# Preparing one attention head at a time in the front of a two-layer cross-attention and feed-forward kernel: key and query side by side, one transpose for both

## What is computed

```python
# x: (2, 1024, 256), ctx_768: (2, 77, 192); 4 heads of 64
ln = layernorm(layernorm(x), ln_l_g, ln_l_b)            # "latents", 1024 tokens
xn = layernorm(ctx, ln_x_g, ln_x_b)                     # context, 77 tokens
q  = ln @ Wq.T
kv = concat([xn @ Wkv.T, ln @ Wlkv.T], axis=1)          # keys and values of 77 + 1024 tokens
k, v = kv[..., :256], kv[..., 256:]
qn, kn = rmsnorm(q, qn_g) * 64**-0.5, rmsnorm(k, kn_g)  # per head, over its 64 numbers
attn = softmax(where(mask, einsum('bhid,bhjd->bhij', qn, kn), -max))
x = x + einsum('bhij,bhjd->bhid', attn, v) @ Wo.T + bo
# then: x + ffn0(norm(x)); x + attention1(norm(x), ctx); x + experts(norm(x)), 8 experts
```

## Time and profile before

| | us |
|---|---|
| median of 3 runs | 837.75 |
| lowest, highest | 835.34, 842.58 |
| span of the profiled execution, first to last instruction | 832.3 |
| TensorE busy, VectorE busy | 766.2, 534.6 |
| ScalarE busy, GpSimd busy | 396.6, 303.0 |

### The profile page before, as it was taken

One profiled execution on the slowest core, in us unless ns is written; L12 is line 12 of the kernel. 1 busy time (PEld: TensorE's weight loads), 2 busy tenths in 40 slices (PEclk: granted clock), 3 DMA queues, 4 the chain that ended last, 5 costly groups with the idle time before them and its releaser, 6 DMA issues.

```text
span 832.3 us, 12982 instructions
## 1 busy us (share of the span) xinstructions
PE 766.2 (92%) x4971; PEld 627.0 (75%) x4971; DVE 534.6 (64%) x1148; ACT 396.6 (48%) x694; POOL 303.0 (36%) x275
## 2 busy tenths in 40 slices
PE   7899889999999999999999989984689999999996
PEld 7765546756656555579979888883689999999996
DVE  7777784576676684266454589985747755666551
ACT  3555443464455334564381345433035765557561
POOL 5511002100211023047371142334335767666673
PEclk9999999999999999999999999996899999999999
DMA  7000000000000100010021201120212445444532
GB/s 184 2 1 0 1 0 1 1 1 1 0 1 1 52 2 1 7 45 3 2 61 37 102 1 52 51 76 27 102 32 71 134 108 147 133 90 104 139 38 27
DMA packets 20359, 38.28 MB, mean 46 GB/s; under 512 B 4786, under 2 KB 15754, under 8 KB 17994
## 3 DMA queue, kind: packets, MB, share of 16 engines
q1 hardware_dynamic: 13641, 29.02, 10.7%
q0 software_dynamic: 6656, 8.43, 6.0%
HBM read 28.91 MB, written 8.40 MB: 45 GB/s over the span
## 4 chain that ended last, share of the span: by engine, by line
PE 60%; DVE 16%; ACT 4%; issue 3%; POOL 2%; DMA 0%; ACTq 0%; DVEq 0%
PE ps L464 19%; PE ps L1148 12%; PE ps L626 9%; PE ps L730 5%; PE ps L647 2%; PE ps L648 2%; PE ps L588 2%; DVE rep L1743 1%; DVE sm L1544 1%; DVE Pb L1548 1%; PE ps L1088 1%; PE ps L1076 1%; DVE sm L1553 1%; PE ps L563 1%; PE ps L798 1%
## 5 line engine op out<-in xcount | busy, mean ns | idle before, releaser
L626 PE MATMUL ps<-PT,VA 128*65 128x512 f32 (+1 forms) x288 | 147.5, 594 | 1.7 <-ACT PT L2035 1.3
L2035 ACT ACTIVATE PT<-ps 128x512 f32<-128x512 f32 x128 | 75.7, 592 | 63.4 <-PE ps L648 63.4
L1148 PE MATMUL ps<-he,wh 128*128 128x258 f32 x768 | 104.1, 288 | 0.0
L464 PE MATMUL ps<-GT,wh 128*128 128x258 f32 x768 | 96.4, 284 | 0.4 <-DVE GT L1841 0.4
L1148 PEld LDWEIGHTS ps<-he,wh 128*128 128x128 f32 x768 | 95.4, 189 | 0.4
L464 PEld LDWEIGHTS ps<-GT,wh 128*128 128x128 f32 x768 | 93.3, 189 | 0.6 <-issue 0.6
L2634 POOL DMA_INDIRECT out_dram<-ye,idx x40 | 64.1, 1603 | 22.6 <-DVE ye L1853 12.0
L1871 DVE TENSOR_TENSOR he<-het,he 128x516 fp32r<-128x516 f32 x64 | 44.6, 697 | 41.4 <-ACT he L1899 40.8
L2388 POOL TENSOR_TENSOR ssq<-ssq,half 128x8 f32<-128x8 f32 x16 | 26.1, 1638 | 122.6 <-DVE ssq L1269 122.6
L647 PE MATMUL ps<-QA,KA 128*128 128x512 f32 x144 | 68.5, 476 | 0.4 <-ACT QB L1899 0.4
L588 PE MATMUL ps<-KA,QA 128*128 128x368 f32 x192 | 59.7, 418 | 3.8 <-DVE x L1353 2.9
(11 more groups left out here) (286 smaller groups left out, 1556.0 us busy)
## 6 DMA issues: line engine op xcount, KB each, us to landing
wr<-in_w1e_dram SPq DMA_DIRECT2D x8, 1024.0 KB, 4.9
wr<-in_w2e_dram SPq DMA_DIRECT2D x8, 1024.0 KB, 4.8
x<-in_x_dram SPq DMA_DIRECT2D x4, 512.0 KB, 6.7
w<-in_w_dram SPq DMA_DIRECT2D x2, 1024.0 KB, 5.0
y_dram<-yr SPq DMA_DIRECT2D x3, 512.0 KB, 3.0
out_dram<-x SPq DMA_DIRECT2D x3, 512.0 KB, 4.1
gt<-y_dram,idx POOLq DMA_INDIRECT x40, 3.3
out_dram<-ye,idx POOLq DMA_INDIRECT x40, 3.9
```

The costliest lines, as they stand in the source:

```text
L464: op = pe.matmul(o, l, r, start=n == 0, stop=n == len(calls) - 1)
L626: pe.matmul(bank[6 + hf][0:65, :], VA[b][0:K, kt, h, :], PT[u % 4][0:K, :], start=kt == 0, stop=kt == 8).then_inc(p_pv, 1)
L1148: op = pe.matmul(bank[dc][:, 0:258], w2h[i][:, wc_], he[j][:, m, 258 * c:258 * c + 258], start=n == 0, stop=n == 23)
L2035: a.activation(PT[u % 4][0:K, :], bank[4 + u % 2][0:K, :], ACT.Exp, bias=0.0 if K == 128 else mcol[:, b:b + 1]).then_inc(a_exp, 1)
```

## The change

The query-key weights are laid out by head: key 0, query 0, key 1, query 1. `normalised` writes each head's key and query once, side by side, so one transpose of a 128x128 tile turns both: the key comes to partitions 0 to 63, the query to 64 to 127 of one bank. A head has two groups of four transposes in place of four. ScalarE's `high_k` copies 64 partitions, and `high_q` is two copies of 64 partitions each, to both halves of QA. VectorE's `low_q` reads partitions 64 to 127, `low_k` writes there from 0 to 63. The context's keys (`kcn`) are written once; a column of zeros stands behind the last head.

In the front head 0 alone is squared, summed and normalised, two token tiles at a time, straight from the bank; the raw numbers of head 1 are copied to `qkr`. Head 1 is squared in one piece behind the last of head 0's first four maxima, its root taken by GpSimd in one piece of 16 columns, and its preparation is the first side work of pass 0, whose SIDE_RATE goes from 1.2 to 1.5. The two runs of `warm` are gone. The value weights are split ahead of the squares, on ScalarE and on GpSimd. `wqk_in[1]` signals d_f.

```diff
-SIDE_RATE = (1.2, 1.4, 1.4, 1.0, 1.0, 1.0, 1.0, 1.0)
+SIDE_RATE = (1.5, 1.4, 1.4, 1.0, 1.0, 1.0, 1.0, 1.0)
...
-        qkn = RP("qkn", [128, 8, 4, 2, DH])
-        kcn = RP("kcn", [SC, H0, 2, DH])
+        qkn = RP("qkn", [128, 8, 2, 2, DH])
+        kcn = RP("kcn", [SC, H0 + 1, DH])
...
-        RA = Arena(RP.at)
+        RA = Arena(RP.at + 8960)
...
+            def turn_head(h, gi, m):
+
+                for t in range(4):
+                    op = pe.transpose(bank[m][:, 128 * t:128 * t + 128],
+                                      qkn[:, 4 * gi + t, h % 2, :, :].rearrange("p a d -> p (a d)"), ident[:, :])
+                op.then_inc(p_ht, 1)
...
             def head(b, h, pick):
...
+                    m = pick(2 * gi)
+                    clear(m)
+                    if H == 1:
+                        pe.wait_ge(v_init, 2)
+                    else:
+                        pe.wait_ge(v_qkn, 2 * (H // 2) + gi + 1)
+                    turn_head(h, gi, m)
+                    busy[m] = (v_qb, 2 * H + 2) if gi else (v_kx, H + 1)
+                    yield
...
-            ctx_product(0, 0, 1)
-            warm(6, 12)
+            pe.wait_ge(a_cT, 1)
+            pe.wait_ge(d_gg, 128)
+            ctx_half(0, slice(0, 256))
+            busy[0] = (v_kcn, 1)
             pe.wait_ge(v_qkn, 1)
             clear(6)
-            turn_head(0, 0, 0, 6)
-            busy[6] = (v_qb, 1)
-            clear(7)
-            turn_head(0, 0, 2, 7)
-            warm(1, 12)
+            turn_head(0, 0, 6)
+            ctx_half(1, slice(256, 512))
...
+            def second_squares():
+
+                v.wait_ge(a_raw, 5)
+                mean_square(0, 8, 1, sq[:, :, :].rearrange("p a (t j d) -> p (a t) j d", t=4, j=2)).then_inc(v_mc, 1)
+
+            def second_normalised():
+
+                v.wait_ge(g_rc, 2)
+                v.tensor_tensor(qkn[:, :, 1, :, :], qkr[:, :, :].rearrange("p a (t j d) -> p (a t) j d", t=2, j=2),
+                                of_head(2, 0, 8, 1).unsqueeze(3).to_broadcast([128, 8, 2, DH]), ALU.mult).then_inc(v_init, 1)
+                yield
+                yield
...
-            beside = [spaced(second, proj(0, 1, False), head(0, 2, side)), spaced(head(0, 3, side), ln(1), ctx(1, 3)),
+            beside = [spaced(second_normalised(), head(0, 1, side), proj(0, 1, False), head(0, 2, side)), spaced(head(0, 3, side), ln(1), ctx(1, 3)),
...
             def high_q(H, gi, m):
-                a.wait_ge(p_ht, 4 * H + 2 * gi + 1)
-                copy(QA[:, H % H0, 512 * gi:512 * gi + 512], bank[m]).then_inc(a_qa, 1)
+
+                h, c = H % H0, slice(512 * gi, 512 * gi + 512)
+                a.wait_ge(p_ht, 2 * H + gi + 1)
+                copy(QA[64:128, h, c], bank[m][64:128, :])
+                copy(QA[0:64, h, c], bank[m][64:128, :]).then_inc(a_qa, 1)
...
             factors(("ctx", 0), 0, 1, SC)
+            low(wv[1], wv_in, wv[0], 2)
...
-            proj(0)
+            for q in range(4):
+                g_.wait_ge(v_ms, q + 1)
+                roots_of_head(2 * q, 2, 0).then_inc(g_rq, 1)
             root_c(0)
-            low(wv[1], wv_in, wv[0], 2)
             low(wqk[1][:, :, 256:512], wqk_in[1], wqk[0][:, :, 256:512], 3)
+            g_.wait_ge(v_mc, 2)
+            roots_of_head(0, 8, 1).then_inc(g_rc, 1)
             low(wo[1], wo_in, wo[0], 4)
```

More of the change, by code:

```diff
@@ L957, in tensor_program @@
                 if qt < 3:
-                    values(0, qt + 1, 7 - qt % 2)
-                if qt > 1:
-                    next(second)
+                    values(0, qt + 1, (7, 6, 7)[qt])
             first_row()
-            next(second)
-            beside = [spaced(second, proj(0, 1, side, False), head(0, 2, side)), spaced(head(0, 3, side), ln(1, side), ctx(1, side)),
+            pe.wait_ge(v_qb, 1)
+            beside = [spaced(idle(2), head(0, 1, side), proj(0, 1, side, False), head(0, 2, side)), spaced(head(0, 3, side), ln(1, side), ctx(1, side)),
                       spaced(proj(1, 0, side, True), head(1, 0, side)), spaced(head(1, 1, side)),
@@ new lines, in of_head, with mean_square, first_squares @@
+            def of_head(row, t0, n, h):
+                return ssq[:, row, 4 * t0:4 * t0 + 4 * n].rearrange("p (t j) -> p t j", j=4)[:, :, 2 * h:2 * h + 2]
+            def mean_square(t0, n, h, src):
+                sums, means = (of_head(row, t0, n, h) for row in range(2))
+                step(v.tensor_reduce(sums, src, AX.X, ALU.add))
+                settle()
+                return v.tensor_scalar(means, sums, 1.0 / DH, 1e-16, ALU.mult, ALU.max)
+            def first_squares(q):
+                v.wait_ge(a_sq, q + 1)
+                src = sq[:, q // 2, 256 * (q % 2):256 * (q % 2) + 256]
+                mean_square(2 * q, 2, 0, src.rearrange("p (t j d) -> p t j d", t=2, j=2)).then_inc(v_ms, 1)
@@ L2225, in scalar_program @@
             affine(1, 1, 7, tsp2[1])
+            halved(wv[0], wv_in, (d_wv, 16))
             for q in range(3):
-                squares(q)
+                first_squares(q)
             ctx_turned(0, 0)
-            squares(3)
-            halved(wv[0], wv_in, (d_wv, 32))
+            first_squares(3)
             ctx_squares(0, 0)
-            ctx_values(0, 1)
-            halved(wqk[0][:, :, 256:512], wqk_in[1], (d_wv, 32))
-            high_q(0, 0, 6)
-            a.wait_ge(v_init, 1)
-            a.wait_ge(p_ht, 2)
-            high_k(0, 0, 7)
-            again_k(0, 0)
-            a.wait_ge(p_ht, 3)
-            copy(KA[:, 0, 512:1024], bank[3], gg[:, 2:3]).then_inc(a_ka, 1)
-            a.wait_ge(p_ht, 4)
-            copy(QA[:, 0, 512:1024], bank[4]).then_inc(a_qa, 1)
-            high_ctx(0)
-            again_k(0, 1)
-            values(0, 0, 6)
-            a.wait_ge(g_wo, 1)
-            halved(wo[0], wo_in, (d_rows, 64))
-            second = head(0, 1, side)
-            for j in (1, 2):
-                values(0, j, 8 - j)
-            next(second)
+            a.wait_ge(v_init, 1)
+            high_k(0, 0, 6)
+            high_q(0, 0, 6)
+            high_k(0, 1, 3)
+            high_ctx(0)
+            ctx_values(0, 1)
+            high_q(0, 1, 3)
+            again_k(0, 0)
+            values(0, 0, 2)
+            again_k(0, 1)
+            values(0, 1, 7)
+            second_squares()
+            halved(wqk[0][:, :, 256:512], wqk_in[1], (d_f, 16))
+            values(0, 2, 6)
             values(0, 3, 7)
@@ L2254, in scalar_program @@
             copy(QB[64:65, 0, 0:512], bank[0][64:65, :], -1.0).then_inc(a_mrt, 1)
-            next(second)
-            next(second)
-            beside = [spaced(second, proj(0, 1, side, False), head(0, 2, side)), spaced(head(0, 3, side), ln(1, side), ctx(1, 3)),
+            a.wait_ge(g_wo, 1)
+            halved(wo[0], wo_in, (d_rows, 64))
+            beside = [spaced(idle(2), head(0, 1, side), proj(0, 1, side, False), head(0, 2, side)),
+                      spaced(head(0, 3, side), ln(1, side), ctx(1, 3)),
                       spaced(proj(1, 0, side, True), head(1, 0, side)), spaced(head(1, 1, side)),
@@ L2388, in proj, with roots_of_head @@
                     g_.tensor_tensor(ssq[:, 2, c], ssq[:, 1, c], half[:, 0:8], ALU.pow).then_inc(g_rq, 1)
+            def roots_of_head(t0, n, h):
+                out_, in_ = (ssq[:, row, 4 * t0:4 * t0 + 4 * n].rearrange("p (t j) -> p t j", j=4)[:, :, 2 * h:2 * h + 2]
+                             for row in (2, 1))
+                return g_.tensor_tensor(out_, in_, half[:, 0:2 * n].rearrange("p (t j) -> p t j", j=2), ALU.pow)
             def low(dst, src, high, n):
```

193 lines of the change are left out of this document (91 added, 102 removed).

## The result

The changed kernel takes 844.74 us (median of 8 runs, 843.26 to 849.83), the kernel before beside it 838.01 us (8 runs, 835.34 to 842.58). The ratio on record for the runs side by side is 1.0092, with a 95% interval of 1.0071 to 1.0114: slower by some 7.7 us. The two medians alone give 1.0080, 6.7 us. The prediction was 2.5 us faster, 835.2, in a range of 829 to 841.

What follows compares the result with a forecast made beforehand. TensorE was taken to bound the passes, roots and VectorE the first 31 us. Terms -2.8 -0.4 +3.6 -4.3 +3.0 -1.6 = -2.5 us took the span from 832.3 to 829.8, the median to 835.2; range 829 to 841.

Steps and rivals of the forecast that it cites:

- The front: Up to pass 0: first maximum 2.8 us earlier, then 0.4 us off, so pass 0 starts 3.2 us earlier.
- Units 0 to 5 of pass 0: Head 1's root, then its normalisation held by GpSimd's split of wo, delay maxima: a loss of 3.6 us.
- Rival (1): Nothing holds the normalisation or the front's latents: pass 0 loses 1.1 us, front gains 3.6; 832.0 us; chance 0.19.
- the clock full for the first 60 us: TensorE's granted clock was expected at 1.00 throughout the first 60 us.
- The heads 2 to 7: TensorE saves 12 transpose groups, 4.3 us, against 3.0 us of new waits for exps: net 1.3 us gained.
- the 6 us: Sign of a wrong forecast: TensorE's waits for exps costing over 6 us, where about 3 were expected.
- Rival (3): ScalarE's three-copy block bounds units with a group: 0.65 us at each of 14 groups, 9.1 us; 841.3 us; chance 0.13.
- Rival (2): The exps aren't late, so the 3.0 us of new waits stay away: 832.2 us; chance 0.14.
- The 1.6 us from shorter normalisations: VectorE's six normalisations of a pair fall to about half, sparing TensorE waits of 1.6 us (0 to 3.5).
- what it costs I count in the 0.25 us: Pass 0's higher rate packs side work into fewer units; its cost was put inside 0.25 us of exp waits per group.
- within 1%: The changed kernel's time lies within 1%, 8.4 us, of the kernel before; chance 0.85.

Runs made afterwards that it cites:

- e1: The changed kernel with ScalarE's copy of the first value product moved ahead of head 0's second query half; ratio 1.0058 to the kernel before.
- e4: The changed kernel with 20 transposes of the identity in unit 2 of pass 0, ahead of the maximum that waits; ratio 1.0087 to the kernel before.
- e3: The changed kernel with the query's second high-part copy left out for heads 4 to 7; ratio 1.0066 to the kernel before.
- e7: The changed kernel with the third copy of each group put off by one side step on ScalarE; ratio 1.0039 to the kernel before.
- e5: The kernel before with only the side-step rate of pass 0 raised from 1.2 to 1.5; ratio 1.0036 to the kernel before.
- e13: The changed kernel with the rate of pass 0 at 1.4 in place of 1.5; ratio 1.0074 to the kernel before.
- e15: Changed kernel with value product copied earlier, split held, sum earlier, third copy put off; head 1's normalisation ahead of pass 0, rate 1.5; ratio 0.9980 to before.
- e16: The kernel of e15 with the rate of pass 0 at 1.3 in place of 1.5; 841.08 us, ratio 0.9946 to the kernel before.
- e2: The changed kernel with GpSimd's split of wo held until head 1's normalisation is over; ratio 1.0070 to the kernel before.

## Why the prediction was wrong, point by point

**The front.** Forecast: first maximum at 27.9, pass 0 at 37.7. The chain of the roots was mis-sized by 0.95 us: "the last of the four end at about 24.05" had each root wait for nothing but VectorE's queue. But VectorE's sums waited for ScalarE's squares, and these waited 0.76 and 0.77 us for TensorE's projections. So the keys were ready at 28.74 us. The step that failed by more is "I get 3.85 us: first maximum at 27.9": it followed the keys alone and did not ask which banks the maximum writes. e1 shows that the bank of the first value product cost 2.6 us; with it mended, pass 0 starts at 38.55, 2.4 us ahead of before, where 3.2 were forecast.

**Units 0 to 5 of pass 0.** Forecast: unit 6 at 14.75 us, a loss of 3.6; measured 16.26, a loss of 5.1 by the same reckoning. Root, split and hold were right, and 1.2 of the 1.5 us missed are the slow clock behind the hold, by e4's profile. Rival (1), no hold, fell. The forecast had the clock full for the first 60 us; it was 0.83 from 50 to 60.

**The heads 2 to 7.** The slots saved are real, 4.3 us, and so is the mechanism that eats them, but "I take 0.25 us of new waits for each of 12 groups, 3.0 us" was mis-sized: the waits for exps grew by 7.5 us. That is over the 6 us which the prediction itself named as a sign of being wrong, and it is the largest single miss. Of the 7.5 us, 1.2 at 74.44 us belong to the packing; the other 6.3 are 0.45 for each of the 14 groups. Rival (3) says that it decides from 0.46 us a group on, but that is 5.5 us over 12 groups; over its own 14 it is 0.39, and 0.45 lies above it. It had a chance of 0.13. Leaving a copy out took 3.3 us off these waits (e3), putting it off 4.4 us (e7), of which 1.1 came back as waits for the context's keys. The working had the numbers for it: an exp done at 2.5 us against 2.2 to 2.3, and against 1.4 in an empty unit. Rival (2), no late exps, fell.

The 1.6 us from shorter normalisations came, nearly whole. (Six times half of 2.29 is 6.9 us of VectorE, not 6.6.) The wait of 0.91 us in the earlier trace rows is gone, as the normalisation ahead of it takes 1.22 us in place of 2.28, and so is one of 0.55 us at 238.23 in the trace of before:

```profile
174.79 1.22 DVE L1270 TENSOR_TENSOR qkn<-qkr,ssq 128x1024 f32<-128x1024 f32 x1
...
176.66 0.78 PE L595 MATMUL ps<-KA,QA 128*128 128x368 f32 x3
```

**The packing of pass 0.** The other step that failed is the sentence "what it costs I count in the 0.25 us". On the kernel before, e5 puts the rate of 1.5 at 0.36% of the time, 3 us, and 4.4 us of pass 0, with 2.5 us of waits among them behind a normalisation that the changed kernel has at half the length. In the changed kernel one place shows 2.2 us of it, and the rate of 1.4 gives 2.8 us of pass 0 back and takes 0.9 in pass 1 (e13). The rate is not a tuning value beside the change: the chain of head 1, moved behind the first scores, brings two empty steps and the steps of `head` that stood ahead of pass 0, 26 in all. At 1.2 only 21 fit into the 18 units, at 1.4 all but the last, which is empty. e15 to e16 show the reverse, 4.7 us of pass 0 back when the chain is out and the rate down.

**The sum.** Up to the last scores -2.5 us was forecast and +8.6 measured. The difference of 11.1 is 3.3 of the front, 1.5 of the units 0 to 5, and 6.2 of everything behind. Of the 6.2 the exps are 4.5; no single row accounts for the rest, and as 3.1 of the 8.8 us of exps' waits lie in pass 0, the exps and the packing can't be added up as two terms. As a time it is +7.7 us by the ratio and +6.7 by the medians, in place of -2.5; the answer "within 1%", at 0.85, held, and the range did not. The rest of the program, whose code is unchanged, does not add to it in a way that could be shown: from the last scores to the end it took 484.6 us before, 488.0 after, and 492.6 in e5, which differs from before by one number in pass 0.

## What to carry to other kernels

Work taken from the engine that is full is worth its slot only if no engine in order behind it gets a longer block ahead of what the full engine needs next: count the block in the shortest unit, not the engine's share of busy time. A rate that deals side work out is part of the cost of whatever makes it necessary, and its price is the waits of in-order queues: look for a side step that waits for another engine (here ScalarE's copy for VectorE's normalisation) and for what stands behind it. One profile is one execution: read its granted clock before two of them are compared. When a product is given another bank, ask who writes that bank next and where the copy that empties it stands in its queue.

## What the runs showed of the hardware

TensorE's granted clock fell to half behind waits, but not behind all of them. In the changed kernel TensorE was busy for 1.21 and 1.07 us of the windows 72 to 74 and 74 to 76 us, and the clock stayed full; in e5 it was busy for 1.44 and 0.43 us from 68 to 72, and the windows behind that were at 0.65 and 0.50:

```profile
68.00:70.00 2.00, 1.44 (x6) 1.00 0.00 0
70.00:72.00 2.00, 0.43 (x1) 1.00 0.00 0
72.00:74.00 2.00, 1.63 (x7) 0.65 0.00 0
74.00:76.00 2.00, 2.00 (x5) 0.50 0.00 0
```

In e2 a projection of 12 matmuls fell into such a stretch and took 2.59 us by its row in place of 1.69 in the changed kernel. The price of a wait can then be more than the wait, here 0.9 us more.

```profile
74.99 2.59 PE L465 MATMUL ps<-wqk,xt 128*128 128x256 f32 x12
```
